# Mamba stage of a decoder kernel: rows of B spread by DMA, four decay banks, the front by channel halves, silu sessions moved

## The reference, cut to what matters

```python
xz = x @ in_proj_w                      # x already rms-normalised; 128 -> 2 x 256
xi, z = jnp.split(xz, 2, axis=-1)
xc = conv(xi)                           # 4 taps along the sequence, per channel
xi = silu(xc + conv_b)
dbc = xi @ x_proj_w                     # 64 rank + 16 B + 16 C
delta = softplus(dbc[..., :64] @ dt_proj_w + dt_proj_b)
A = -exp(A_log)
def step(h, inp):                       # over 512 positions; 256 channels x 16 states
    h = exp(d_t[..., None] * A) * h + (d_t * x_t)[..., None] * B_t[:, None, :]
    y = einsum('ben,bn->be', h, C_t)
y = (ys + D_skip * xi) * silu(z)
h1 = x + y @ out_proj_w
```

## Time and profile before

| what | us |
|---|---|
| runs, median of 3 (lowest to highest) | 1243.81 (1240.3 to 1244.13) |
| the profiled execution, its own time | 1240.69 |
| its span | 1238.4 |
| Mamba stage in it, to the last residual's end | 174.5 |

### The profile page before, as it was taken

The page is one execution under the profiler, slowest core; times in us unless marked ns, Lnnn a source line. Parts: engine busy times, 40 slices in busy tenths (PEclk is TensorE's granted clock), DMA queues, the critical chain, the costliest instruction groups (busy, mean ns, idle before and its releaser), DMA issues. The chain is left out here.

```text
span 1238.4 us, 26336 instructions
## 1 busy us (share of the span) xinstructions
PE 1132.5 (91%) x9652; PEld 720.1 (58%) x9652; DVE 945.4 (76%) x1385; ACT 850.9 (69%) x1363; POOL 649.4 (52%) x522
## 2 busy tenths in 40 slices
PE   7786869999776899999999999999999999999975
PEld 2222337777533576666766676666666676667651
DVE  1788957777554788887888788887888788887843
ACT  4554435666453588777877888688877787787844
POOL 1655623454252676664657565655656565656520
PEclk9888978999996899999999999999999999999998
DMA  3000007110020364354535453445435353534310
GB/s 116 1 1 0 1 17 222 52 51 1 5 97 18 97 159 101 99 127 110 125 84 129 105 143 92 105 114 134 101 96 135 102 127 87 129 97 118 94 50 17
DMA packets 75510, 107.11 MB, mean 86 GB/s; under 512 B 25347, under 2 KB 31938, under 8 KB 75002
## 3 DMA queue, kind: packets, MB, share of 16 engines
q1 hardware_dynamic: 75386, 105.47, 32.6%
HBM read 30.89 MB, written 0.59 MB: 25 GB/s over the span
## 5 line engine op out<-in xcount | busy, mean ns | idle before, releaser
L1691 POOL TENSOR_TENSOR st_sq_sum<-h 128x512 f32<-128x512 f32 x96 | 122.1, 1272 | 224.0 <-ACT h L1448 223.2
L1695 POOL TENSOR_TENSOR mo_w<-mo_w,x 128x512 f32<-128x512 f32 x96 | 122.6, 1278 | 101.9 <-DVE x L1566 101.9
L1580 DVE SCALAR_TENSOR_TENSOR st_turned<-banks,mo_w 128x1024 f32<-128x1024 f32 x96 | 117.5, 1224 | 72.0 <-ACT banks L1459 38.6
L1448 ACT ACTIVATE h<-banks 128x512 f32<-128x512 f32 x192 | 114.5, 597 | 71.5 <-PE banks L1291 67.2
L1311 PEld LDWEIGHTS banks<-st_wv,stream 128*128 128x128 f32 x768 | 100.8, 192 | 45.1 <-issue 44.4
L1352 PEld LDWEIGHTS banks<-st_p_blocks,st_vs 128*64 128x64 f32 x1536 | 81.6, 137 | 78.0 <-issue 73.2
L1697 POOL TENSOR_TENSOR mo_w<-mo_w,x 128x512 f32<-128x512 f32 x96 | 122.5, 1276 | 0.0
L430 POOL TENSOR_TENSOR ma_dbx<-ma_u,ma_b_rows 128x1024 f32<-128x1024 f32 x32 | 75.4, 2357 | 76.0 <-ACT ma_b_rows L288 52.0
L1480 ACT ACTIVATE st_p_blocks<-banks 64x512 f32<-64x512 f32 x192 | 112.0, 583 | 3.2 <-PE banks L1340 0.8
L1704 POOL TENSOR_TENSOR mo_w<-st_prob,st_ri 128x512 f32<-128x512 f32 x96 | 100.4, 1046 | 15.0 <-DVE st_ri L1666 15.0
L1299 PE MATMUL banks<-st_sq_sum,head_ones 128*128 128x512 f32 x192 | 101.1, 609 | 6.9 <-POOL st_sq_sum L1691 6.8
(11 more groups left out here) (238 smaller groups left out, 2752.7 us busy)
## 6 DMA issues: line engine op xcount, KB each, us to landing
st_qT<-st_turned SPq DMA_DIRECT2D x192, 128.0 KB, 2.3
st_k_blocks<-st_turned SPq DMA_DIRECT2D x384, 64.0 KB, 2.0
st_vs<-st_vn SPq DMA_DIRECT2D x96, 192.0 KB, 2.5
st_w_raw<-in_w_qk SPq DMA_DIRECT2D x12, 512.0 KB, 4.9
st_vs<-st_vn SPq DMA_DIRECT2D x96, 48.0 KB, 2.1
mo_w_all<-gate_rows SPq DMA_DIRECT2D x1, 3072.0 KB, 13.1
st_wv<-in_w_v SPq DMA_DIRECT2D x12, 256.0 KB, 3.0
st_wo<-in_wo SPq DMA_DIRECT2D x12, 256.0 KB, 3.0
```

The costliest lines, as they stand in the source:

```text
L1448: A(sq[:, part, :], ps[:, part, :], ACT.Square).then_inc(sq_done.sem, 1)
L1580: v.scalar_tensor_tensor(turned[:, h % 4], NORM_BANK.unsqueeze(1).to_broadcast([P, 2, SEQ]), 1e12, cos_part[:, which], ALU.min, ALU.mult). ...
L1691: nc.gpsimd.tensor_tensor(sq_sum[:], sq[:, 0, :], sq[:, 1, :], ALU.add).then_inc(sq_summed.sem, 1)
L1695: nc.gpsimd.tensor_tensor(cos_part[:, which, 0, :], cos_part[:, which, 0, :], sin_part[:, 1, :], ALU.subtract).then_inc(add_done.sem, 1)
```

## The change

`select` shrinks to the C half. The 16 rows of B are copied by ACT once per batch, from PSUM into `b_flat` on partitions 64 to 79, and SP issues one DMA per item that reads one partition of it and writes all 128 of `b_rows`, now a ring of four. `spread_b` and `copy_b` are gone, and bank 6 becomes a fourth decay bank. In the front, low-rank product, softplus, delta, u and item 0's dbx go by halves; the loads of `in_w`, `taps`, `rms_w` and `pick` are issued from ACT's queue, before its first table load; PE gets 10 products of a zeroed bf16 tile before the means and 8 behind them. z of both batches and x of batch 1 are copied raw from PSUM (`raw`), through bank 3 or 4, and their silus are made later from SBUF in sessions of their own: x of batch 1 after item 3, z of batch 0 after item 16, z of batch 1 after item 23. POOL makes u of batch 1 and the gate product of batch 0. The tail of batch 1 goes by halves.

```diff
+    B_RING = 4
...
+    DECAY, SPARE, SUM, C_BANK = (0, 1, 2, 6), 3, 4, 7
...
+    BANK = dict(x00=2, x01=3, z00=4, z01=5, x10=3, x11=4, z10=3, z11=3)
...
+        for i in range(ITEMS):
+            b, n = divmod(i, STATES)
+            sp.wait_ge(b_flat_done.sem, b + 1)
+            if i >= B_RING:
+                sp.wait_ge(dbx_done.sem, 2 * (i - B_RING + 1))
+            sp.dma_start(b_rows[:, i % B_RING, :], b_flat[64 + n:65 + n, b, :].unsqueeze(1).to_broadcast([1, P, SEQ])).then_inc(b_in[i % B_RING].sem, 16)
...
+        def busy(n):
+            for _ in range(n):
+                mm(ps[:, C_BANK, :], still[:, 0:P], still[:], start=True, stop=True)
...
+        pe.wait_ge(still_done.sem, 1)
+        busy(10)
...
         mean(1)
+        busy(8)
...
+            convolved(0, k)
         pe.wait_ge(small_in.sem, 64)
         low_rank(0, 6)
+        gate_proj(0, 0)
...
             step_size(0, k, k)
...
         spread_c(0)
+        gate_proj(0, 1)
...
+        pe.wait_ge(silu_done.sem, 2)
+        convolved(1, 0)
+        pe.wait_ge(raw_done.sem, RAW["z00"])
+        convolved(1, 1)
...
+            if i == 4:
+                pe.wait_ge(raw_done.sem, RAW["z11"])
+                low_rank(1, SPARE)
+            if i == 7:
+                pe.wait_ge(dt_copied.sem, 2)
+                pe.wait_ge(low_done.sem, 2)
+                pe.wait_ge(b_flat_done.sem, 2)
+                step_size(1, 0, SPARE)
+            if i == 11:
+                pe.wait_ge(delta_done.sem, 3)
+                step_size(1, 1, SPARE)
+            if i == STATES + 4:
+                pe.wait_ge(delta_done.sem, 4)
+                out_proj(0)
             if i + 1 < ITEMS:
                 spread_c(i + 1)
             add_state(i)
...
+        ac.dma_start(in_w[:], d["in_w"]).then_inc(front_in.sem, 16)
+        ac.dma_start(taps[:].rearrange("p i k c -> p (i k c)"), bass.AP(d["taps"].tensor, 0, [[0, P], [1, 8 * P]])).then_inc(front_in.sem, 16)
+        ac.dma_start(rms_w[:], d["rms1"]).then_inc(front_in.sem, 16)
+        ac.dma_start(pick[64:128], d["pick"]).then_inc(pick_in.sem, 16)
...
+        def raw(which):
+            to = (xc if which[0] == "x" else sz)[:, int(which[1]), int(which[2]), :]
+            ac.wait_ge(front_done.sem, FRONT[which])
+            A(to, ps[:, BANK[which], :], ACT.Copy).then_inc(raw_done.sem, 1)
...
+        def flat(b, bank):
+            A(b_flat[64:64 + STATES, b, :], ps[64:64 + STATES, bank, :], ACT.Copy).then_inc(b_flat_done.sem, 1)
...
+                if j >= 4:
+                    ac.wait_ge(scan_done.sem, j - 3)
+                A(ps[:, DECAY[j % 4], :], delta[:, b, k, :], ACT.Exp, scale=a_neg[:, k, n:n + 1]).then_inc(decay_done.sem, 1)
...
+        def activated(which, at):
+            nc.scalar.preload_act_table_set("silu_and_others")
+            ac.wait_ge(raw_done.sem, RAW[at])
+            if which == "x1":
+                for k in range(2):
+                    A(xc[:, 1, k, :], xc[:, 1, k, :], ACT.Silu, bias=chan[:, k, 0:1]).then_inc(silu_done.sem, 1)
+            else:
+                b = int(which[1])
+                A(sz[:, b], sz[:, b], ACT.Silu).then_inc(silu_done.sem, 1)
+            nc.scalar.preload_act_table_set("natural_log_exp_and_others")
...
+        flat(0, 6)
+        magnitude(0, 0)
+        decline(0, 0)
+        magnitude(0, 1)
+        log_of(0, 0)
+        decline(0, 1)
+        log_of(0, 1)
...
         decay(0)
...
+        raw("z00")
+        raw("z01")
         for i in range(1, ITEMS):
             decay(i)
...
+            if i == 1:
+                raw("x10")
+                raw("x11")
+            if i in (2, 3):
+                raw(("z10", "z11")[i - 2])
+            if i == 3:
+                activated("x1", "x11")
+            if i == 7:
                 high(1, SPARE)
...
+                flat(1, SPARE)
+            if i in (10, 13):
+                magnitude(1, i // 13)
+                decline(1, i // 13)
+            if i in (11, 14):
+                log_of(1, i // 14)
+            if i == 16:
+                activated("z0", "z01")
+            if i == 23:
+                activated("z1", "z11")
...
+        def step_sizes(b, k):
+            dv.wait_ge(softplus_step.sem, (4, 6, 9, 12)[2 * b + k])
+            v.scalar_tensor_tensor(delta[:, b, k, :], ps[:, SPARE if b else k, :], 0.0, mag[:, b, k, :], ALU.max, ALU.add).then_inc(delta_done.sem, 1)
...
+            dv.wait_ge(dbx_done.sem, 2 * i + (k + 1 if i == 0 else 2))
...
+        for k in range(2):
+            step_sizes(0, k)
+            dv.wait_ge(delta_done.sem, k + 1)
+            dv.wait_ge(silu_done.sem, k + 1)
+            v.tensor_tensor(u[:, 0, k, :], delta[:, 0, k, :], xc[:, 0, k, :], ALU.mult).then_inc(u_done.sem, 1)
...
+            if i == 6:
+                rank_copy(1, SPARE)
+            if i == 7:
+                low_part(1, SPARE)
+            if i == 10:
+                step_sizes(1, 0)
+            if i == 13:
+                step_sizes(1, 1)
+            if i == STATES + 1:
+                for k in range(2):
+                    skip(0, k)
+            if i == STATES + 6:
                 residual(0)
...
+        for k in range(2):
+            skip(1, k)
+            dv.wait_ge(gate_step.sem, 5 + 2 * k)
+            dv.wait_ge(silu_done.sem, 6)
+            v.tensor_tensor(gated[:, 1, k, :], gated[:, 1, k, :], sz[:, 1, k, :], ALU.mult).then_inc(gate_step.sem, 1)
...
+        def step_times_x(k):
+            pool.wait_ge(delta_done.sem, 3 + k)
+            pool.wait_ge(silu_done.sem, 3 + k)
+            nc.gpsimd.tensor_tensor(u[:, 1, k, :], delta[:, 1, k, :], xc[:, 1, k, :], ALU.mult).then_inc(u_done.sem, 1)
...
+            if i == 12:
+                step_times_x(0)
+            if i == 16:
+                step_times_x(1)
+                pool.wait_ge(u_done.sem, 4)
+            pool.wait_ge(b_in[i % B_RING].sem, 16 * (i // B_RING + 1))
...
+            if i == 0:
+                for k in range(2):
+                    pool.wait_ge(u_done.sem, k + 1)
+                    nc.gpsimd.tensor_tensor(dbx[:, 0, k, :], u[:, 0, k, :], b_rows[:, 0, :], ALU.mult).then_inc(dbx_done.sem, 1)
+            else:
+                nc.gpsimd.tensor_tensor(dbx[:, i % 3], u[:, b], b_rows[:, i % B_RING, :].unsqueeze(1).to_broadcast([P, 2, SEQ]), ALU.mult).then_inc(dbx_done.sem, 2)
+            if i == STATES + 3:
+                pool.wait_ge(gate_step.sem, 2)
+                pool.wait_ge(silu_done.sem, 5)
+                for k in range(2):
+                    nc.gpsimd.tensor_tensor(gated[:, 0, k, :], gated[:, 0, k, :], sz[:, 0, k, :], ALU.mult).then_inc(gate_step.sem, 1)
```

More of the change, by code:

```diff
@@ L125, in build_mamba @@
     ITEMS = 2 * STATES
+    FRONT = {name: i + 1 for i, name in enumerate(("x00", "x01", "z00", "z01", "x10", "x11", "z10", "z11"))}
+    RAW = {name: i + 1 for i, name in enumerate(("z00", "z01", "x10", "x11", "z10", "z11"))}
+    BANK = dict(x00=2, x01=3, z00=4, z01=5, x10=3, x11=4, z10=3, z11=3)
     @block.sync
@@ L188, in add_state @@
                 if b == 0:
[L189 removed]
+                    pe.wait_ge(raw_done.sem, RAW["x11"])
                 else:
@@ L236, in _ @@
             add_state(i)
[L237 to L248, removed]
+            if i in (0, 1):
+                pe.wait_ge(raw_done.sem, RAW[("x10", "z10")[i]])
+                gate_proj(1, i)
         pe.wait_ge(h1_done.sem, 1)
@@ L265, in _ @@
         nc.scalar.preload_act_table_set("silu_and_others")
[L267 to L272, removed]
-                A(sz[:, b, k, :], ps[:, gate_bank[k], :], ACT.Silu).then_inc(silu_done.sem, 1)
         ac.wait_ge(small_in.sem, 64)
-        silu(0, 2, (4, 5))
+        for k in range(2):
+            ac.wait_ge(front_done.sem, FRONT[f"x0{k}"])
+            A(xc[:, 0, k, :], ps[:, BANK[f"x0{k}"], :], ACT.Silu, bias=chan[:, k, 0:1]).then_inc(silu_done.sem, 1)
         nc.scalar.preload_act_table_set("natural_log_exp_and_others")
         A(a_neg[:], a_log[:], ACT.Exp).then_inc(a_step.sem, 1)
+        def raw(which):
+            to = (xc if which[0] == "x" else sz)[:, int(which[1]), int(which[2]), :]
+            ac.wait_ge(front_done.sem, FRONT[which])
+            A(to, ps[:, BANK[which], :], ACT.Copy).then_inc(raw_done.sem, 1)
         def high(b, bank):
@@ L308, in _ @@
[L308 to L315 removed]
+                if n == 0:
+                    ac.wait_ge(delta_done.sem, 2 * b + k + 1)
@@ new lines, in decay @@
+                if j == 2:
+                    ac.wait_ge(silu_done.sem, 1)
+                if j == 3:
+                    ac.wait_ge(low_done.sem, 1)
+                if j >= 4:
+                    ac.wait_ge(scan_done.sem, j - 3)
+                A(ps[:, DECAY[j % 4], :], delta[:, b, k, :], ACT.Exp, scale=a_neg[:, k, n:n + 1]).then_inc(decay_done.sem, 1)
+        STEP = {(0, 0, "abs"): 1, (0, 0, "exp"): 2, (0, 1, "abs"): 3, (0, 0, "ln"): 4, (0, 1, "exp"): 5, (0, 1, "ln"): 6,
```

(20 more changed lines are left out.)

128 lines of the change are left out of this document (25 added, 103 removed).

## The result

The changed kernel takes 1376.7 us, median of 4 runs (1374.7 to 1377.5), against 1244.0 for the kernel before beside it: ratio 1.106, 95% interval 1.103 to 1.109. The forecast was 1223; what came is rival B.

A forecast was written before the change was run, and what follows sets the result against it. The prediction took DVE to bound the late scan loop, with waits along PE, ACT and DVE; gains of 8.1 (front), 8.8 (loop) and 2.1 us (tail) sum to 19.0, giving 1223 us, range 1212 to 1244.

The forecast's parts named there:

- rival B: Scan loop: B rows land too slowly, at the upper bound 12.0 us each, Mamba ending at 417.5, 1484 us; chance 0.16.
- Rows of B by DMA: Scan loop: 32 transfers of 256 KB from one SBUF partition each, hidden if one lands per 3.36 us.
- the lower end: B row transfer time taken for the forecast: 1.2 us for 256 KB, from an SBUF-to-SBUF copy at 219 GB/s.
- upper bound: B row transfer time kept as a rival: 12.0 us, from 34 KB out of 16 partitions at 22 GB/s.
- point of decision: B row pace from which the kernel would be slower than before: 3.95 us per row.
- The front: Before the second item's scan: that scan starts at 31.9 instead of 40.00, 8.1 us gained.
- T: Front: end of the first batch's convolutions, at 18.0 instead of about 20.5 us.
- The loop: Scan loop from the second item: 117.7 us including 7.6 of stalls, last product ending at 149.6; 8.8 us gained.
- stall of 2.4 before item 3: Early loop: PE, slow after idling, delays a raw copy and so the decay of item 3; 2.4 us lost.
- Rival C: Scan loop: PE falls to half clock, DVE waits 1.4 us per item, 1244 us if in 15 items; chance 0.07.
- The tail: After the last product: skip and gate by halves, 5.9 us to the residual instead of 8.0, 2.1 gained.
- The sum: Whole Mamba stage: gains of 8.1 in front, 8.8 in loop and 2.1 in tail, 19.0 us.

The follow-up runs named there:

- half rows: Changed kernel, each DMA bringing only the first 256 of 512 columns of its B row, used twice: 1239.8 us, ratio 0.996.
- order of states: Changed kernel with the 16 states taken as 0, 4, 8, 12, 1, ..., so rows in flight lie in different groups of four partitions: 1258.2 us, ratio 1.011.
- rows from HBM: Changed kernel, but ACT's flat B rows are stored to HBM once per batch and each row is spread from there: 1223.5 us, ratio 0.985.
- three banks: Changed kernel with B rows spread from HBM, and three decay banks instead of four: 1223.4 us, ratio 0.985.
- session after item 5: Changed kernel with B rows spread from HBM, and the silus of batch 1's x after item 5 instead of item 3: 1218.1 us, ratio 0.980.
- fewer products: Kernel with B rows from HBM and batch 1's x silus after item 5, with 4 instead of 8 products behind the means: 1216.3 us, ratio 0.977.
- without the added products: Changed kernel with B rows spread from HBM, and the 18 added TensorE products removed: 1227.3 us, ratio 0.987.

## Why the prediction was wrong, point by point

**Rows of B by DMA: the step that failed.** It said "I take the lower end, whose row is nearest in kind": 1.2 us for 256 KB, from 219 GB/s in the earlier trace rows. Measured: 9.6 us for most rows and 8.4 in the mean, and 31 x 8.4 is 261 us of loop. What the two kinds of row have in common (SBUF to SBUF, the bytes) is not what decides; how many source partitions the bytes come out of does: 96 and 32 in the earlier trace rows, one here. The half rows (4.8 us apart) and the order of states (4.5) show both sides of this. That the 22 GB/s of the earlier trace rows lie so near to 27 is luck. With rows from HBM, 32 KB out of the 16 partitions of `b_flat` land in 1.6 and 2.9 us, and the rows' 256 KB in 3.1, so a short transfer's landing time is no rate. The Trainium skill (SBUF — State Buffer, section on the DMA port swizzle) gives 27.6 GB/s for partitions 0 to 3; the trace agrees for reads, with 256 KB in 9.63 us, 27.2 GB/s, and most slices above at 23 to 33 GB/s. That page's rule was weighed and given too little. The mechanism of rival B was right, with its size between the bounds: first row at 33.4 (33.7 worked out from the upper bound), 8.4 per row instead of 12.0. Its point of decision, 3.95 us per row, was a little low: at 4.07 (half rows) the kernel still gains 3.7 us, where the rival's sum has it lose about as much, and at (175.4 - 32.7) / 31 = 4.60 (order of states) it loses 14.6. That some of the stalls which the forecast adds up hide under the wait for a row would explain this; it was not measured.

**The front** held: T at 18.0 forecast, 18.02 measured. With rows from HBM `u` of half 0 ended at 25.60 (26.15 forecast), and POOL began at 26.18, held by the first row by then:

```profile
26.18 1.27 POOL L495 TENSOR_TENSOR ma_dbx<-ma_u,ma_b_rows 128x512 f32<-128x512 f32 x1 [16.02 <-DMA ma_b_rows<-b_line]
```

The second `u`, taken to end at 28.2, ended at 28.00, and the second item's scan stood at 31.76 (31.9). POOL's start on the forecast's 26.2 is in part luck: `u` was 0.55 us early and the row from HBM as late.

**The loop** held, with its rows in time: the wait in front of item 4's decay was 3.89 (3.9 forecast), the one for the spread of C 1.43 (1.3); from 56 to the last product DVE waited once, 0.37. The sessions after items 16 and 23 and POOL's products did hide. The stall of 2.4 before item 3 is missing in this trace. It rested on PE's clock falling after its gap, as in the earlier trace rows; here PE had idled 3.04 us and its spread still took 0.47. In three other kernels with rows from HBM the clock fell after that gap, and the stall came: 1.75 us with three banks, 1.83 with the session after item 5, 1.84 with fewer products. So the step was right in kind, and the stall comes in one trace and not in the next. The last product ended at 148.1 (149.6 forecast): 2.4 less for that stall, and 0.9 more elsewhere. Rival C did not come: 20.00 of 20 us from 120 to 140 are DVE's, at a granted clock of 1.00.

```profile
120.00:140.00 20.00, 14.29 (x31) 5.04 (x30) 20.00 (x18) 8.30 (x12) 14.15 (x6) 1.00 0.14 36
```

**The tail** was 5.98 us with rows from HBM (5.9 forecast) and 6.25 in the changed kernel. **The sum** of 19.0 was 20.4 in the trace (174.52 to 154.12) and 20.0 in the medians with rows from HBM. Where only the source of one transfer differs, the forecast of 1223 meets 1223.5. To the half microsecond that is luck, since the later stages alone vary by more. For the kernel as changed the forecast missed by 154 us.

**What stays open**: why four groups read in turn give 59 GB/s and not four times 27; why the last row of a group lands 3.7 us after the third; and why the clock falls after a gap of 3.0 us in one trace and not in another.

## What to carry to other kernels

Price a DMA by the partitions that it reads as well as by its bytes: in this kernel one SBUF partition spread over 128 costs some 9.6 us per 256 KB, and the same bytes by way of HBM land in 3.1 us. Where one term of a sum has bounds a factor of ten apart and is issued 32 times, that term is the forecast; give it a chance by mechanism, not by the row that looks alike. And before work moves into a loop, ask whether the engine that takes it has lead: the same order of work lost 15 us with the copy of B in ACT's queue (and `select` at full width) and gained 9 on top of the rows without it.

## What the runs showed of the hardware that was not expected

- Transfers out of one group of four partitions moved 27 GB/s (33 in the mean from 60 to 100 us, with the changes of group) while the DMA engines showed 86% busy; the order of states moved 59 at 88%. The busy share does not tell the rate. The issuing instruction is held as well: an issue took 9.5 us in the median on SP's queue, and 0.32 with rows from HBM.
- DVE's product of two SBUF operands took 0.69 us with POOL idle (changed kernel, 26.30) and 1.76 beside POOL's (rows from HBM, 26.24), the same instruction with the same data. There POOL's product had begun 0.06 us earlier. With the session after item 5 DVE began first (26.19 against 26.31): its product took 0.69, and POOL's two took 2.93 instead of 2.48.
- In five traces with rows from HBM PE idled 2.99 to 3.05 us at the same place in the loop. The four sums behind took 1.98 us in two of them (the first, and the one without the added products) and 3.03 to 3.68 in the other three. One gap of 2.39 in the kernel before was followed by a slow spread as well. The length of a gap alone does not say what the clock does.
